# One accumulating transfer of 1 MB for a group of eight probability tiles, rows of 8192 bytes, in place of two of 512 KB

## What is computed

```python
e = leaky_relu(u[:, None] + v[None, :])      # one score per pair of nodes
e = where(adj > 0, e, NEG_BIG)
att = softmax(e, axis=1)                     # needs the sum of exp over each row: the denominator
h = elu(att @ Wh)
```

## Time and profile before

| | |
|---|---|
| median of 3 runs | 3445.28 us (3441.72 to 3446.64) |
| the profiled execution's own time | 3447.01 us |
| its span, first to last instruction | 3445.2 us |
| TensorE's mean granted clock | 0.981 |
| busy share of the span | PE 90%, DVE 83%, ACT 66%, POOL 8% |
| share of the 16 DMA engines: q1, q0 | 51.2%, 16.2% |

### The profile page before, as it was taken

The page is one execution under the profiler, slowest core; times in us unless marked ns, Lnnn a source line. Parts: engine busy times, 40 slices in busy tenths (PEclk is TensorE's granted clock), DMA queues, the critical chain, the costliest instruction groups (busy, mean ns, idle before and its releaser), DMA issues. The chain is left out here.

```text
span 3445.2 us, 56585 instructions
## 1 busy us (share of the span) xinstructions
PE 3096.8 (90%) x21977; PEld 1071.2 (31%) x21977; DVE 2865.5 (83%) x5292; ACT 2274.0 (66%) x3934; POOL 280.9 (8%) x330
## 2 busy tenths in 40 slices
PE   1479999999999999699999999997999999999998
PEld 0123333333333333233333333332333333333333
DVE  5468888888888876699999999997888788888886
ACT  0247776666766767477777777784666666666665
POOL 0000000000000000000000000001112112211211
PEclk9989999999999999899999999998999999999999
DMA  8999999999999981221312222214667766766764
GB/s 242 287 346 342 342 338 338 335 341 333 342 341 332 342 259 55 86 86 64 112 71 105 79 96 87 88 62 135 166 158 166 188 155 161 178 167 163 170 150 80
DMA packets 441759, 679.29 MB, mean 197 GB/s; under 512 B 297474, under 2 KB 318082, under 8 KB 416914
## 3 DMA queue, kind: packets, MB, share of 16 engines
q1 hardware_dynamic: 409458, 564.40, 51.2%
q0 software_dynamic: 32032, 111.27, 16.2%
HBM read 430.10 MB, written 77.69 MB: 147 GB/s over the span
## 5 line engine op out<-in xcount | busy, mean ns | idle before, releaser
L1235 DVE SCALAR_TENSOR_TENSOR eps<-ua,v8col,cb 128x512 f32<-128x512 f32 x2800 | 1963.9, 753 | 294.5 <-ACT prob L630 218.4
L630 ACT ACTIVATE prob<-eps,v2col 128x512 f32<-128x512 f32 x2392 | 1526.2, 689 | 599.1 <-PE eps L810 588.9
L851 PE MATMUL acc<-prob,feat 128*64 128x512 f32 x4784 | 1216.5, 605 | 6.4 <-ACT acc_s L638 6.4
L810 PE MATMUL eps<-nt,nbig 128*64 128x512 fp8e4 (+2 forms) x6642 | 997.5, 385 | 150.7 <-DVE eps L1235 146.5
L810 PEld LDWEIGHTS eps<-nt,nbig 128*64 128x64 bf16 (+2 forms) x6642 | 327.7, 103 | 1032.0 <-DVE eps L1235 687.7
L851 PEld LDWEIGHTS acc<-prob,feat 128*64 128x64 f32 x4784 | 305.9, 137 | 381.7 <-issue 208.0
L1065 DVE TENSOR_SCALAR mi<-stage 128x1024 uint8<-128x1024 int32 x512 | 351.7, 688 | 66.4 <-DMA stage<-in_adj_dram 66.0
L630 ACT ACTIVATE mi<-eps,v2col 128x512 f32<-128x512 f32 x344 | 219.5, 687 | 102.0 <-PE eps L810 100.3
L630 ACT ACTIVATE stage<-eps,v2col 128x512 f32<-128x512 f32 x336 | 214.6, 687 | 95.1 <-PE eps L810 93.4
L860 PE MATMUL den<-prob,ones 128*32 128x512 f32 x2048 | 275.5, 610 | 0.0
L1074 DVE TENSOR_SCALAR edges<-nt 128x2048 int32<-128x2048 int32 x192 | 234.0, 1219 | 29.7 <-PE misc L821 15.2
(11 more groups left out here) (175 smaller groups left out, 1810.4 us busy)
## 6 DMA issues: line engine op xcount, KB each, us to landing
stage<-in_adj_dram SPq DMA_DIRECT2D x512, 512.0 KB, 6.8
nt<-nt_d SPq DMA_DIRECT2D x128, 1024.0 KB, 6.1
nt_d<-nt SPq DMA_DIRECT2D x64, 1024.0 KB, 7.1
prob<-prob POOLq DMA_DIRECT2D x64, 512.0 KB, 5.8
mi<-mi POOLq DMA_DIRECT2D x64, 512.0 KB, 6.4
stage<-stage POOLq DMA_DIRECT2D x64, 512.0 KB, 6.6
ub<-u_d SPq DMA_DIRECT2D x48, 256.0 KB, 5.2
xy_d<-xin POOLq DMA_DIRECT2D x32, 256.0 KB, 3.3
```

The lines of the kernel that those rows point to most:

```text
L630: nc.scalar.activation(weights(l, b, j), eps[:, j % ES, :], ACT.Exp, bias=v2col[:, j:j + 1]).then_inc(s_p, 1)
L810: mm = nc.tensor.matmul(et[c:c + cols, :], nbig[:, c:c + cols], edge, start=False, stop=True, skip_group_check=True, tile_position=(0, c))
L851: mm = nc.tensor.matmul(acc[h:h + C, :], feat[:, l % 2, j, 0:C], weights(l, b, j), start=(k == 0), stop=(k == NT // 2 - 1))
L1235: dv.scalar_tensor_tensor(eps[:, j % ES, :], ua[:, par, :], v8col[:, j:j + 1], cb[:, par, :], ALU.add, ALU.max).then_inc(s_fill, 1)
```

## The change

One transfer takes the place of two: it adds tiles 4 to 7 of a group onto tiles 0 to 3, in rows of 8192 bytes. It waits for the last pair of the group, as the second transfer of before did. PE waits for one semaphore in place of two, and its four matmuls read tiles 0 to 3 in place of 0, 1, 4, 5. Three semaphores serve in turn in place of six.

```diff
-ADDS = 6
+ADDS = 3
...
-        def added(b, g, h):
+        def added(b, g):
 
-            n = 2 * (b * len(ADDED) + ADDED.index(g)) + h
-            return s_two[n % ADDS], 16 * (n // ADDS + 1)
+            n = b * len(ADDED) + ADDED.index(g)
+            return s_four[n % ADDS], 16 * (n // ADDS + 1)
...
             def add_probs(b, g):
 
-                for h in range(2):
-                    pool.wait_ge(s_main, group(2, b, 4 * g + 2 * h + 1) + 1)
-                    buf, o = places(b, DEN * g + QUAD * h)
-                    nc.gpsimd.dma_start(buf[:, o:o + 2, :], buf[:, o + 2:o + 4, :], accum_op=ALU.add).then_inc(
-                        added(b, g, h)[0], 16)
+                pool.wait_ge(s_main, group(2, b, 4 * g + 3) + 1)
+                buf, o = places(b, DEN * g)
+                nc.gpsimd.dma_start(buf[:, 0:QUAD, :], buf[:, QUAD:DEN, :], accum_op=ALU.add).then_inc(
+                    added(b, g)[0], 16)
...
                 if g in ADDED:
-                    for h in range(2):
-                        pe.wait_ge(*added(b, g, h))
-                rounds = ((0, 1, 4, 5),) if g in ADDED else ((0, 1, 2, 3), (4, 5, 6, 7))
+                    pe.wait_ge(*added(b, g))
+                rounds = ((0, 1, 2, 3),) if g in ADDED else ((0, 1, 2, 3), (4, 5, 6, 7))
```

More of the change, by code:

```diff
@@ L263, in build @@
         s_den = sem("probs_in_denominators")
-        s_two = [sem(f"probs_added_by_two{i}") for i in range(ADDS)]
+        s_four = [sem(f"probs_added_by_four{i}") for i in range(ADDS)]
         s_setup = sem("setup_steps")
```

## The result

The changed kernel takes 3455.24 us (median of 7 runs, 3452.60 to 3459.43) against 3445.11 us of the kernel before (7 runs, 3441.72 to 3446.64): a ratio of 1.0033, 95% interval 1.0021 to 1.0044. It is 10.1 us slower. That is inside the range on record and clear of the 0.2% that the prediction called no change, so the likeliest case, "in effect no change", was not the one that came; its own range, 3440 to 3454 us, was missed by 1.2 us. The profiled execution has a span of 3456.7 us, 11.5 more than before.

The account below looks back on a forecast made before the run. The prediction took a nearly always busy PE to bound the kernel, with accumulating transfers on its path. Late group 0 landings of 2.4 and 1.0 us, all else 0, added 3.4 to 3445.3: 3448 us, range 3432 to 3500 us.

Parts of the forecast that it names:

- in effect no change: Whole kernel: likeliest case, 3448 us, own range 3440 to 3454 us, chance 0.48.
- the most to be had: Third layer: PE's waits for accumulating transfers, 15.4 us in 13 pieces, the most an edit to them can give back.
- PE's waits for `den` near 18.8 us: Sign over the third layer: 15.4 + 3.4 us of waits expected; a total far from that means the prediction is wrong.
- First block, +2.4 us: Group 0, first block: sharing engines with a mask load, it lands some 9.9 us after issue; PE waits 2.4 us.
- Eleventh block, +1.0 us: Group 0, eleventh block: landing goes from 6.4 to 9.2 us against a use after 8.15; PE waits 1.0 us.
- Undisturbed landing, 7.4 us: Quiet group 0: 1 MB lands 1.8 + 5.56 = 7.4 us after issue, in place of 4.6.
- Group 0's margin: Group 0 in a block: landing after 7.4 us, use 8.2 us after issue, 0.8 us to spare.
- Group 3: it lands when it did, 0: Group 3, all 13 places: full engines do the same work, so landing and PE's 1.49 us wait stay; 0 change.
- A wait put on PE there costs most of its length: Steady third layer: PE is busy 380.4 of 400 us, so an added wait costs most of its length in time.
- wide packets are dearer: Rival, groups 0 and 3 of each block: wide accumulating packets cost more; 3477 to 3521 us, chance 0.24.
- Larger turns: Rival, group 3: double-size packets give q0 two thirds of the work, landing it earlier; at most 15.4 us, 3430 us; chance 0.16.
- Group 0 late in every block: Rival, step 23 of each block: a small delay exceeds 0.8 us; with 1 us over, 15 us, 3460 us; chance 0.07.

Follow-up runs that it names:

- e1: Changed kernel with group 3 alone back to two 512 KB transfers in rows of 4096 bytes; +7.6 us against the kernel before, ratio 1.0025.
- e2: Changed kernel with each group's 1 MB transfer made of two rows of 4096 bytes per partition; +22.6 us against the kernel before, ratio 1.0064.
- e6: Changed kernel with the first two mask loads of a block in the third layer issued earlier, at steps 24 and 32; 3432.15 us.
- e8: Changed kernel with two halves as before in the first block and in group 3 of every block; 3450.2 us, ratio 1.0015.
- e9: Changed kernel with the first two mask loads earlier and the first block's groups in two halves as before; 3431.44 us.
- e7: Kernel before with the first two mask loads of a block in the third layer issued earlier, at steps 24 and 32; 3430.20 us.
- e5: Kernel before with group 3 alone added by one 1 MB transfer, the other groups in two halves; +6.0 us, ratio 1.0017.
- e3: Kernel before with both 512 KB halves of every group issued only after the group's last pair; 3457.5 us, ratio 1.0040.
- e4: Changed kernel with each group's transfer split into two of 64 partitions, rows of 8192 bytes; +204.6 us against the kernel before, ratio 1.0596.

## Why the prediction was right, and where not

The chain was read rightly: 8.6 of the 11.5 us between the two profiled executions are PE's waits for these transfers. Without the meeting with the mask loads the kernel before takes 14.2 us less, close to the 15.4 us that the prediction named as the most to be had, and the changed kernel about 22 us less. The range held the time in part by luck: its upper part stood there for dear packets, and these did not come. A sign of being wrong that the prediction had named did come: it wanted PE's waits for `den` near 18.8 us, and they are 24.0. The forecast of no change was wrong, by these steps:

- *First block, +2.4 us.* Right in sum, 1.4 + 0.75 us, and in part by chance: group 0 landed after 8.8 us, not 9.9, and the rest is at group 1, which was taken as in time. Group 4 was taken as in time too, and waited 0.7 us in the last block.
- *Eleventh block, +1.0 us.* The size was right by luck, the place wrong: group 0 had 1.3 us to spare in that block and waited 1.0 us in the third. The places are not random. In the third block all six kernels that add group 0 in one transfer (changed, e1, e2, e6, e8, e9) land it late, after 9.1 to 9.4 us, and wait 1.0 to 1.2 us; the late eleventh block of before comes again in e7 (6.3 us). In these third blocks one packet of a queue `instruction` stands within the transfer's time. That it delays the transfer is not shown: in other blocks there is one and no delay. PE's matmul in the changed kernel, and the queues from 2516 to 2525.5 us:

```profile
2525.31 1.06 PE L881 MATMUL den<-mi,ones 128*32 128x512 f32 x8 [1.03 <-DMA mi<-mi]
...
q0 software_dynamic: 222, 1.69, 88.3%
q8 instruction: 1, 0.02, 0.6%
```

- *Undisturbed landing, 7.4 us.* 6.9 us; the wide packets save 6% per byte. Group 0's margin was 1.3 us in most blocks, not 0.8.
- *"Group 3: it lands when it did, 0."* This is the step that failed. Group 3 lands 0.4 us later, and in thirteen blocks that is 4.7 us of added waits (20.1 in place of 15.4). The prediction held the work of both queues to be the same. Counted packet by packet over these blocks, group 3's own packets take 5.0 us of all engines in place of 5.2, but those of the two mask loads 6.5 in place of 6.05; the first packet of group 3 starts 5.2 us after the first issue in place of 4.8. With one transfer the mean landing was 13.61 to 13.96 us in three kernels, with two it was 13.30 to 13.46 in four. How much of the 4.7 us belongs to the single transfer is less sure: the four kernels with halves in group 3 wait 15.4, 16.7, 17.4 and 17.3 us there, those with one transfer 18.4, 20.1 and 22.9, each in one execution. Rows of 4096 bytes do not help. Why the loads' packets last longer beside the single transfer, and why it starts later, these runs do not show.
- *"A wait put on PE there costs most of its length."* Too low. The kernels without earlier loads, ordered by PE's waits, are also in order of time but for e8 and e5, which lie within 1.1 us of each other: e5, 3.0 us more waits than before and 6.0 us; e8, 4.0 and 4.9; e1, 5.8 and 7.6; changed, 8.6 and 10.1; e3, 11.2 and 13.0; e2, 15.8 and 22.6. The clock can be part of the rest: a spell of 6.8 us is 3.4 us of PE's work at full speed, and the changed kernel's 23.9 us more of low clock are an estimated 11.9 us of PE work at most, less where PE would have waited anyway. But this share is not shown. e3 and e8 have fewer low spells than the kernel before, none of them in the steady blocks, and still cost 1.2 times their added waits, as the changed kernel does. The number of spells may also differ from one execution to the next: the mean granted clock of the changed kernel's seven runs goes from 0.977 to 0.982.

The rivals: *wide packets are dearer* is refuted as it was put, 4.96 against 5.30 us per MB. The row met the Trainium skill's limit of 2048 elements per such operation (DMA: Bandwidth & Descriptors, section on what the DMA engines do beyond copying) exactly, and its packets show no price for it. The slower time that this rival stood for came by another way. *Larger turns* brought no time to group 3: q0 and q1 shared the engines (45.5% and 56.4%), and when group 3's megabyte was through, q1 had sent 255 or 256 of the 256 packets of its two loads in all thirteen blocks, as the prediction's count of turns had it. The turns did hold the loads back: the last of their packets ends 11.8 us after POOL's first issue (mean), before it was 9.2. *Group 0 late in every block* did not come, one block apart. By the rule of the Trainium skill for a transfer issued from GpSimd (the same page, section on the anatomy of one DMA issued from GpSimd) 1 MB would land after an estimated 4.4 us; the accumulating one here took 6.9 us, and the measurement decides.

## What to carry to other kernels

Merging two transfers into one saves issues and a few per cent of engine time, and takes away the first half's head start: before doing so, list for each place the time from the last half's issue to its use, and compare it with the landing of the whole. Where a transfer that is waited for meets bulk loads, look for another time for the loads before working on the transfer: moving two loads that nobody was waiting for 6 and 14 steps ahead gave 14 us, where the change itself took 10. And price a new wait on a busy TensorE above its length: here each added microsecond of waits went with 1.2 to 2 us of time, in kernels without low clock in the steady blocks too.

## What was not expected of the hardware

- An accumulating transfer over 64 partitions takes 9.3 us of all 16 engines per MB, one over 128 partitions with the same rows of 8192 bytes 4.96: half the partitions, nearly twice the cost per byte.
- An accumulating SBUF transfer of 1 MB lands 6.9 us after issue with 128 rows of 8192 bytes and 7.9 us with 256 rows of 4096; POOL's issue takes 0.85 and 1.19 us.
- A wait of 2.18 us in a busy stretch was followed by a granted clock of 0.53 for 7 us, in which PE was busy throughout; one of 1.66 us at 3023 us was not, and there the next matmuls of `acc` took 1.08 and 1.03 us. Over all traces but e4's, 13 of the 17 waits of 2 us and more for a transfer had a low spell with them or just behind; e8's wait of 2.54 us had none.
